# Attention's maximum pass as pairs of 64-row products, the second half's keys stored swapped, and one of eight high parts made by VectorE

## What is computed

```python
q = (x @ Wq.T).reshape(b, t, N_HEADS, HEAD_DIM)          # 8 heads of 64
kv_latent = x @ Wkv_down.T                               # 64 latent columns
k = (kv_latent @ Wk_up.T).reshape(b, t, N_HEADS, HEAD_DIM)
v = (kv_latent @ Wv_up.T).reshape(b, t, N_HEADS, HEAD_DIM)
scores = jnp.einsum('bqhd,bkhd->bhqk', q, k) * scale
attn = jax.nn.softmax(scores, axis=-1)
out = jnp.einsum('bhqk,bkhd->bqhd', attn, v)
return out.reshape(b, t, N_HEADS * HEAD_DIM) @ Wo.T
```

## Time and profile before

| | |
|---|---|
| median of three runs (lowest to highest) | 1378.51 us (1374.25 to 1379.99) |
| profiled execution | 1377.57 us |
| its span, first to last instruction | 1375.6 us |
| busy over the span: TensorE, VectorE, ScalarE, GpSimd | 1219.7, 1145.5, 1054.7, 962.1 us |
| attention's loop in the span | from about 502 to 1140 us |

### The profile page before, as it was taken

One profiled execution on the slowest core, in us unless ns is written; L12 is line 12 of the kernel. 1 busy time (PEld: TensorE's weight loads), 2 busy tenths in 40 slices (PEclk: granted clock), 3 DMA queues, 4 the chain that ended last, 5 costly groups with the idle time before them and its releaser, 6 DMA issues.

```text
span 1375.6 us, 30660 instructions
## 1 busy us (share of the span) xinstructions
PE 1219.7 (89%) x10192; PEld 745.8 (54%) x10192; DVE 1145.5 (83%) x3141; ACT 1054.7 (77%) x2351; POOL 962.1 (70%) x1100
## 2 busy tenths in 40 slices
PE   3999999867888879999999999999999999677776
PEld 1455555434455536665666666666666667344443
DVE  6999998589998888888777787877878754799998
ACT  3332333677899869999999989999999995787776
POOL 4456644368777777778777778777777773388887
PEclk9899999989999999999999999999999999799998
DMA  6200000000012000010000000000000000000000
GB/s 174 77 1 1 0 0 1 1 1 1 10 38 78 27 21 25 25 26 25 25 14 14 2 2 2 2 3 2 2 2 2 2 3 1 1 31 16 25 22 32
DMA packets 35529, 25.32 MB, mean 18 GB/s; under 512 B 16358, under 2 KB 32044, under 8 KB 35372
## 3 DMA queue, kind: packets, MB, share of 16 engines
q1 hardware_dynamic: 35372, 23.36, 6.0%
HBM read 14.89 MB, written 8.39 MB: 17 GB/s over the span
## 4 chain that ended last, share of the span: by engine, by line
PE 58%; ACT 13%; issue 12%; DVE 11%; POOL 4%; DVEq 0%; DMA 0%; SPq 0%; POOLq 0%; ACTq 0%
PE banks L2023 7%; PE banks L2025 6%; PE banks L2011 6%; DVE arena L1535 4%; PE banks L1761 4%; PE banks L1969 4%; PE banks L1720 4%; PE banks L2040 4%; PE banks L2041 4%; PE banks L2042 3%; ACT arena L1174 3%; DVE arena L1530 3%; ACT arena L1182 2%; PE banks L1748 2%; PE banks L1776 2%
## 5 line engine op out<-in xcount | busy, mean ns | idle before, releaser
L839 POOL TENSOR_TENSOR arena<-arena 128x512 f16<-128x512 f32 x383 | 437.6, 1161 | 150.5 <-ACT arena L1182 146.6
L1174 ACT ACTIVATE arena<-banks 128x512 f32<-128x512 f32 x512 | 302.9, 599 | 45.5 <-PE banks L2025 40.8
L1611 DVE TENSOR_REDUCE arena<-banks 128x1 f32<-128x512 f32 x512 | 325.8, 680 | 4.0 <-PE banks L2011 1.8
L1182 ACT ACTIVATE arena<-arena 128x512 f16<-128x512 f32 x512 | 316.2, 632 | 0.0
L1530 DVE MAX8 arena<-arena 128x8 f32<-128x256 f32 x512 | 190.4, 414 | 27.4 <-issue 15.9
L2040 PE MATMUL banks<-arena 128*128 128x65 f16 x2016 | 211.4, 193 | 0.9
L2041 PE MATMUL banks<-arena 128*128 128x64 f16 x2016 | 211.5, 195 | 0.0
L2042 PE MATMUL banks<-arena 128*128 128x65 f16 x2016 | 210.6, 193 | 0.0
L1637 DVE TENSOR_TENSOR arena<-arena 128x512 f16<-128x512 f32 x129 | 107.0, 829 | 123.2 <-ACT arena L1182 123.0
L1535 DVE MATCH_REPLACE8 arena<-arena 128x256 f32<-128x256 f32 x512 | 206.2, 411 | 0.9 <-issue 0.2
L2040 PEld LDWEIGHTS banks<-arena 128*128 128x128 f16 x2016 | 187.9, 96 | 31.8 <-issue 9.9
(11 more groups left out here) (229 smaller groups left out, 2545.1 us busy)
## 6 DMA issues: line engine op xcount, KB each, us to landing
arena<-q_store SPq DMA_DIRECT2D x48, 128.0 KB, 2.7
x<-in_L_attn_a_x SPq DMA_DIRECT2D x8, 512.0 KB, 3.9
q_store<-arena SPq DMA_DIRECT2D x32, 128.0 KB, 1.8
out<-x SPq DMA_DIRECT2D x7, 512.0 KB, 2.9
arena<-arena SPq DMA_DIRECT2D x64, 1.0 KB, 1.9
arena<-in_L_attn_a_W_in SPq DMA_DIRECT2D x1, 768.0 KB, 5.8
arena<-in_L_attn_a_W_mid SPq DMA_DIRECT2D x1, 512.0 KB, 7.6
arena<-in_L_attn_a_w_w SPq DMA_DIRECT2D x2, 256.0 KB, 8.0
```

What stands on the lines that cost most here:

```text
L839: nc.gpsimd.tensor_tensor(pr_lo[c][:, kt, :], pr[:, kt, :], pr_hi[c][:, kt, :], ALU.subtract).then_inc(a_lP, 1)
L1174: nc.scalar.activation(pr[:, kt, :], ps[6 + kt % 2][:, :], ACT.Exp, scale=SM_SCALE).then_inc(a_P, 1)
L1182: nc.scalar.activation(pr_hi[c][:, kt, :], pr[:, kt, :], ACT.Copy).then_inc(a_hi, 1)
L1611: nc.vector.tensor_reduce(mx_half[c][:, i // 2, i % 2:i % 2 + 1], ps[n % MAX_BANKS][:, :], X, ALU.max).then_inc(a_mx, 1)
```

## The change

Each two maximum products become a pair, `max_pair(W, j)`, issued in steps 0, 2, 4 and 6. Either product uses 64 of the 128 rows: the first half of the keys in partitions 0 to 63, the second half in 64 to 127. To that end the second half of the keys is stored with high and low parts swapped, so that its high parts are in 64 to 127; the score products, which sum over all rows, are not changed by the order. The maximum is now one of high parts by high parts only. The pair waits once, until the bank of its second product has been read. The latent rows, which are made from the keys by a transpose, are copied in two pieces for the second half to undo the swap. Apart from that the high part of step 3 is made by VectorE (`high`, in step 4 between the reduction and the subtraction) instead of ScalarE, with a semaphore of its own on which GpSimd's subtraction of step 3 waits.

```diff
+        HIGH_DVE = 3
+
+        def high_done(W, kt):
+
+            if kt == HIGH_DVE:
+                return W + 1
+            return W * (KT - 1) + kt + (kt < HIGH_DVE)
...
+        def low_half(c):
+
+            return slice(HD, P) if c == 0 else slice(0, HD)
...
             def low(W, kt):
                 c = W % 2
-                pool.wait_ge(a_hi, W * KT + kt + 1)
+                pool.wait_ge(a_hiD if kt == HIGH_DVE else a_hi, high_done(W, kt))
                 nc.gpsimd.tensor_tensor(pr_lo[c][:, kt, :], pr[:, kt, :], pr_hi[c][:, kt, :],
                                         ALU.subtract).then_inc(a_lP, 1)
...
             def latent(B, c, bank):
                 act.wait_ge(a_lps, B * 2 + c + 1)
-                nc.scalar.activation(lat[B % 2][:, c * TPC:c * TPC + TPC, 1:1 + 2 * HD],
-                                     ps[bank].bitcast(F16)[:, 0:TPC * P].rearrange("p (t d) -> p t d", t=TPC),
+                rows = ps[bank].bitcast(F16)[:, 0:TPC * P].rearrange("p (t d) -> p t d", t=TPC)
+                tiles = slice(c * TPC, c * TPC + TPC)
+                if c == 0:
+                    nc.scalar.activation(lat[B % 2][:, tiles, 1:1 + 2 * HD], rows, ACT.Copy).then_inc(a_l, 1)
+                    return
+                nc.scalar.activation(lat[B % 2][:, tiles, 1:1 + HD], rows[:, :, HD:P], ACT.Copy)
+                nc.scalar.activation(lat[B % 2][:, tiles, 1 + HD:1 + 2 * HD], rows[:, :, 0:HD],
                                      ACT.Copy).then_inc(a_l, 1)
...
                     exps(W, kt)
-                    if kt:
+                    if kt and kt - 1 != HIGH_DVE:
                         high(W, kt - 1)
...
             def keys_low(B, c, bank):
                 cs = slice(c * CH, c * CH + CH)
                 dve.wait_ge(a_k, ((B - AHEAD) * 2 + c) * 2 + 2)
-                nc.vector.tensor_tensor(kA[B % 2][HD:P, cs], ps[bank][HD:P, :], kA[B % 2][HD:P, cs],
+                low = low_half(c)
+                nc.vector.tensor_tensor(kA[B % 2][low, cs], ps[bank][low, :], kA[B % 2][low, cs],
                                         ALU.subtract).then_inc(a_kl, 1)
...
+            def high(W):
+
+                dve.wait_ge(a_P, W * KT + HIGH_DVE + 1)
+                wait_from(dve, a_ops, W - 1)
+                nc.vector.tensor_copy(pr_hi[W % 2][:, HIGH_DVE, :], pr[:, HIGH_DVE, :]).then_inc(a_hiD, 1)
...
                     if W + 2 < ALL:
                         largest_of(W + 2, kt)
+                    if kt == HIGH_DVE + 1:
+                        high(W)
                     if kt in (LAST_DVE if W == ALL - 1 else LOW_DVE):
                         low(W, kt)
...
-            def max_scores(W, i):
+            def max_pair(W, j):
 
                 B, hh, c, slot = place(W)
-                j, half, n = i // 2, i % 2, W * HALVES + i
...
-                wait_from(pe, a_mx, n - MAX_BANKS + 1)
+                wait_from(pe, a_mx, n + 1 - MAX_BANKS + 1)
                 every = qA[:, slot, c * CH:c * CH + CH].rearrange("p (q j) -> p j q", j=TPC)
-                mm(ps[n % MAX_BANKS][:, :], every[:, j, :], kA[B % 2][:, half * CH:half * CH + CH],
-                   start=True, stop=True).then_inc(a_mps, 1)
+                for half in range(2):
+                    high = slice(HD * half, HD * half + HD)
+                    mm(ps[(n + half) % MAX_BANKS][:, :], every[high, j, :], kA[B % 2][high, half * CH:half * CH + CH],
+                       start=True, stop=True).then_inc(a_mps, 1)
...
                     scores(W, kt)
-                    if W + 2 < ALL:
-                        max_scores(W + 2, kt)
+                    if W + 2 < ALL and kt % 2 == 0:
+                        max_pair(W + 2, kt // 2)
```

More of the change, by code:

```diff
@@ L337, in hybrid_block_kernel @@
         a_hi = sem("a_exp_high")
+        a_hiD = sem("a_exp_high_vector")
         a_lD = sem("a_exp_low_dve")
@@ L1210, in head_second @@
                         act.wait_ge(h_kmps, k + 1)
-                        nc.scalar.activation(kA[B][HD:P, c * CH:c * CH + CH], ps[bank][HD:P, :],
+                        low = low_half(c)
+                        nc.scalar.activation(kA[B][low, c * CH:c * CH + CH], ps[bank][low, :],
                                              ACT.Copy).then_inc(a_kl, 1)
@@ L1635, in low @@
                 c = W % 2
-                dve.wait_ge(a_hi, W * KT + kt + 1)
+                dve.wait_ge(a_hi, high_done(W, kt))
                 nc.vector.tensor_tensor(pr_lo[c][:, kt, :], pr[:, kt, :], pr_hi[c][:, kt, :],
                                         ALU.subtract).then_inc(a_lD, 1)
+            def high(W):
+                dve.wait_ge(a_P, W * KT + HIGH_DVE + 1)
+                wait_from(dve, a_ops, W - 1)
+                nc.vector.tensor_copy(pr_hi[W % 2][:, HIGH_DVE, :], pr[:, HIGH_DVE, :]).then_inc(a_hiD, 1)
             def head(t):
@@ L1997, in slot_work @@
                     read[slot] = (s_zT, (LN_ATTN + n * 2 + part[0]) * 2 + part[1] + 1)
-            def max_scores(W, i):
+            def max_pair(W, j):
                 B, hh, c, slot = place(W)
-                j, half, n = i // 2, i % 2, W * HALVES + i
-                if i == 0:
+                n = W * HALVES + 2 * j
+                if j == 0:
                     pe.wait_ge(a_kl, B * 2 + 2)
-                if i == 0 and B < AHEAD:
+                if j == 0 and B < AHEAD:
                     pe.wait_ge(s_qld, (B * NH + hh + 1) * 48)
-                if i == 0 and B >= AHEAD:
+                if j == 0 and B >= AHEAD:
                     pe.wait_ge(a_dup, query_done(W))
-                wait_from(pe, a_mx, n - MAX_BANKS + 1)
+                wait_from(pe, a_mx, n + 1 - MAX_BANKS + 1)
                 every = qA[:, slot, c * CH:c * CH + CH].rearrange("p (q j) -> p j q", j=TPC)
-                mm(ps[n % MAX_BANKS][:, :], every[:, j, :], kA[B % 2][:, half * CH:half * CH + CH],
-                   start=True, stop=True).then_inc(a_mps, 1)
+                for half in range(2):
+                    high = slice(HD * half, HD * half + HD)
+                    mm(ps[(n + half) % MAX_BANKS][:, :], every[high, j, :], kA[B % 2][high, half * CH:half * CH + CH],
+                       start=True, stop=True).then_inc(a_mps, 1)
             def scores(W, kt):
@@ L2101, in head_second @@
                     pe.wait_ge(f_lg, NT)
-                    for i in range(2):
-                        max_scores(0, i)
+                    max_pair(0, 0)
                     pe.wait_ge(*head_read[2])
-                    for i in range(2, HALVES):
-                        max_scores(0, i)
+                    for j in range(1, TPC):
+                        max_pair(0, j)
             ffn(0)
-            for i in range(HALVES):
-                max_scores(1, i)
+            for j in range(TPC):
+                max_pair(1, j)
             pe.wait_ge(f_fs, NT + CREDIT["f_fs"])
```

## The result

The changed kernel takes 1428.48 us (1426.01 to 1429.18), against 1377.57 in the runs beside it: 1.037 times as long, interval 1.034 to 1.039. The forecast was 1381, its range ended at 1397. The profiled execution's span grew from 1375.6 to 1426.9 us, by 51.3. Of that, 45.8 lie in the 64 items of attention's loop: from the first score product of its first step to the first of its last step it lasts 673.8 us, before 628.0. Another 3.4 lie ahead of the loop, which starts at 505.42 instead of 502.00.

A forecast was written before the change was run, and what follows sets the result against it. TensorE was taken to bound the kernel, with ScalarE hardly behind in items without other work. Terms 3.4 - 0.5 - 1.7 + 2.9 - 0.5 = +3.6 us on 1377.57 gave 1381 us; range 1355 to 1397.

The forecast's parts named there:

- The pair's wait: Ahead of a pair, for two of three banks: +0.6 us in about 5 items behind row statistics, +2.9 us.
- Rival C: Wait for two banks, steps 0, 2, 4, 6: pairs wait for VectorE's reductions, +17, 1395 us; chance 0.14.
- The price of a pair: Pair between full-width products, division changing twice: 0.45 us against 0.43, +0.02; +3.4 us in 41 items.
- A: In the pairs: changing the array's division costs nothing, a pair saves 0.2 us, result 1337 us; chance 0.13.
- B: In the pairs: changing the array's division costs half, a pair at 0.34 us, result 1363 us; chance 0.15.
- D: In the pairs: the two halves don't overlap, a pair at 0.67 us, result 1437 us; chance 0.05.
- The high part at 0: VectorE's copy in step 4, 0.44 to 0.83 us, is covered by its idle time before the subtraction: cost 0.
- Items without other work: 17 loop items without queries or output products: -0.1 us each, between -0.31 and +0.08; -1.7 us in all.
- The clock: TensorE's clock at its lower level between 503 and 1153 us, named as a sign of a wrong forecast; unpriced.
- the first two maximum passes: Before 502 us: paced by VectorE's reductions and ending with the same wait, so 0.

The follow-up runs named there:

- the last four kernels: Full products in pairs, subtractions moved (1386.02 us); changed kernel, own bank waits (1425.89); kernel before, VectorE's low part of chunk 6 for 4 (1377.51), plus its high part (1405.87).
- the first experiment: Changed kernel with the high part of step 3 back on ScalarE, pairs kept: 1416.59 us, 1.027 times the kernel before.
- the kernel of 1396.59 us: Changed kernel with all high parts on ScalarE and VectorE's two subtractions moved behind the reductions of steps 2 and 6: 1396.59 us, 1.014.
- the last kernel above: Kernel before with VectorE making the low parts of chunks 0 and 6 instead of 0 and 4, and chunk 6's high part: 1405.87 us, 1.021.

## Why the prediction was wrong

The steps from the kernel before to the changed one, each the difference of two medians: 1377.0 us before (the runs beside the last four kernels); +9.1 for grouping full products in pairs, order mended; +10.6 for making them halves; +20.0 for the order of VectorE's subtractions; +11.9 for the high part on VectorE. Together 1428.5. In the loop of the profiled executions the same four steps are 9.5, 5.4, 21.6 and 9.3, together the 45.8.

*The pair's wait* is the step that failed. It was sized at +0.6 us in 5 items behind row statistics, +2.9 us, on the ground that "in most items the reductions run ahead". The pairs wait 45.2 us, in items of every kind: the kernel with full products in pairs, whose array is never divided, still lost 46 us; 12 of them, by the first experiment, to the high part. The statement "the pair waits where the second waited" was wrong about the time: the second product used to ask for its bank a step later. To let the first product start on its own bank gave back 2.6 us; to ask a step later gave back 26, and to take VectorE's subtractions from ahead of the reductions 20 and 28.5. The earlier trace rows showed single products hardly waiting, not what two at once would need. Rival C had this mechanism and named the threshold (over 25 us on the weight loads; 67.3 came), but at half a reduction of 0.6 us once in an item, +17. Its place was right; its size was a third, since it counted VectorE's added work and not the waits ahead of the reductions.

*The price of a pair* was 0.45 against 0.43 us, +0.02; it is +0.05. The parts that the prediction listed were right: the starts in the kernel of 1396.59 us, where nothing waits, are (lines 2054 and 2056 the score products, 2042 the pair, 1998 the output products)

```profile
663.46 0.38 PE L2056 MATMUL banks<-arena 128*128 128x512 f16 x1
663.77 0.41 PE L2042 MATMUL banks<-arena 64*128 64x512 f16 x2
664.11 1.13 PE L1998 MATMUL banks<-voB,arena 128*128 128x256 f32 x4
665.07 0.38 PE L2054 MATMUL banks<-arena 128*128 128x512 f16 x1
...
665.50 1.03 PE L1998 MATMUL banks<-voB,arena 128*128 128x256 f32 x4
666.37 0.38 PE L2054 MATMUL banks<-arena 128*128 128x512 f16 x1
```

0.31 from the score product to the pair and 0.34 from the pair to the next start; less the 0.215 that the score product streams, the pair takes 0.435, where 0.45 was forecast. But behind the pair come f32 products, in steps 0 and 2 of these items: they take 0.96 us until the next product may start, the same four without a change ahead of them 0.87. This exposed load was read in the earlier trace rows (0.33 for 0.27) and then left out of the sum, which took the f16 weights of the earlier trace rows. The pair of step 0 then costs 0.525; with that of step 2, which has f32 transposes behind it, this is most of the 0.19 an item. The Trainium skill, "TensorEngine Tiling (Array Packing)", Key Properties, says that a change of mode drains TensorE; the 0.1 us on either side agree. Rivals A and B, which gave the change away or half of it, and D, in which the halves don't overlap, fell.

*The high part at 0* failed too: +8 us alone, +12 with the pairs. The cover that was named, VectorE's idle time ahead of its subtraction, is there, but GpSimd is the one that pays: its subtraction of step 3 waited 43 us for the copy, in 61 of the 64 items, and "the next subtraction waits for ScalarE anyway" covers less than half of that. With the copy alone, the subtraction of step 5 still waits 33.9 us for ScalarE, in 40 items, where it waited 53.5 in 46 before. The bound on the copy's time was right in the mean (589 ns, of 414 to 1217; forecast 0.44 to 0.83), from the group of line 1663:

```profile
L1663 DVE CAST arena<-arena x64: 414/577/1217, 512.2 to 1176.8; 128x512 f16<-128x512 f32 x64
```

Neither saving a copy on ScalarE (its busy time in the loop fell) nor the idle of VectorE was worth anything here, as neither was what the items waited for.

*Items without other work*, -0.1 each by forecast, take +0.62. With the order mended, 8.78 with halves and 8.76 with full products: here the division costs nearly nothing, since ScalarE sets the pace, and the bound of +0.08 was exceeded by the pairs' places alone. The remaining 0.22 to 0.24 come at the place where the earlier trace rows show ScalarE waiting 0.26 us for TensorE: in step 4 a pair (0.43 us) now stands ahead of the score products of step 5, where a single product (0.215) stood, and ScalarE waits 0.46 us there with halves (at 571.55) and 0.47 with full products:

```profile
569.05 0.60 ACT L1190 ACTIVATE arena<-banks 128x512 f32<-128x512 f32 x1 [0.47 <-PE banks L2055]
```

*The clock.* The prediction named a lower clock between 503 and 1153 us as a sign that it was wrong, and it came. Busy times after, and TensorE's timeline there:

```profile
665.00:668.00 3.00, 3.00 (x10) 1.18 (x10) 2.10 (x7) 1.98 (x4) 1.59 (x5) 0.50 0.00 0
```

```profile
664.55 0.41 PE L2040 MATMUL banks<-arena 64*128 64x512 f16 x2 [1.95 <-DVE arena L1630]
664.89 0.61 PE L2052 MATMUL banks<-arena 128*128 128x512 f16 x1
665.29 0.63 PE L2054 MATMUL banks<-arena 128*128 128x512 f16 x1
```

Behind a pair's wait of 1.95 us the granted clock is at 0.50, the 1.2 GHz level, for about 3 us, and the next product starts 0.40 us behind the one before it instead of 0.215. This is an item behind row statistics; at 698.03 and 876.09 a wait of 1.95 us has the same behind it. These are the three longest waits of pairs in the loop; the fourth, 1.88 us at 839.99, has no lower clock behind it. Together these stretches are some 10 us at the lower level, which costs at most 5. Before, there is no such stretch from 503 to 1153 us, and with full products and the mended order there is none in the loop after 504. So these three go with the waits; the item at 695.49 lost 2.3 us by both, where +0.6 had been forecast for its kind.

A fourth stretch is older than the pairs' waits. In the changed kernel the clock is at its lower level from 487.4 us, ahead of the first pair at 492.70, to 508; before, it is at 1.00 from 488 to 510.

```profile
503.00:507.00 4.00, 2.74 (x9) 0.54 (x10) 3.75 (x7) 0.45 (x1) 0.00 (x0) 0.50 0.00 0
```

So the first two maximum passes, sized at 0, last 12.7 us up to the loop instead of 9.4. In the kernel with full products in pairs and the mended order, where the clock was at its upper level for most of this stretch, they last 10.0: most of the 3.3 us goes with the clock, and why it fell there is not known.

## What to carry to other kernels

A product that needs two buffers at once has a wait of its own, even if the work is the same: before grouping, go through the queue of the engine that frees the buffers and ask what each freeing instruction stands behind. Where an engine in the middle of a cycle has slack, the slack is no cover for those who wait for it; put its instructions that wait for others behind the ones that release the bound engine, as here, where that order alone gave back 20 and 28.5 us. Whether a fourth bank would have done the same was not tried. Half-array products between full-width ones gave nothing back here: two halves side by side cost 0.05 us more than two full products.

## What the runs showed of the hardware

VectorE and GpSimd disturb each other. In the kernel before, VectorE's subtraction of 512 elements takes 680 to 693 ns in the 38 cases in which no subtraction of GpSimd overlaps it, and 829 in the mean of 129. In the last kernel above, 25 of 129 lie wholly beside GpSimd's, with a median of 1526 ns; the copy from f32 to f16, 412 ns at its fastest, has a median of 953 in 35 cases wholly beside them. VectorE's reductions from PSUM take 680 ns in the mean before and 681 after, and 680 in the median of the 246 that lie wholly beside GpSimd's subtractions.

The records show a wait and not a lower rate. In the last kernel, each of the 80 VectorE subtractions of over 1 us began while one of GpSimd's ran and ended 0.54 to 0.55 us after that one's end (the one at 578.40 above ends at 579.93, and GpSimd's row ends at 579.38). It goes the other way too: 93 of GpSimd's 95 subtractions of over 1.25 us (1.15 at the fastest) began while VectorE's copy or subtraction ran, and ended 1.01 to 1.03 us after its end. The Trainium skill, "SBUF — State Buffer", Who interferes with whom, says that the two engines share a pair of ports as an exclusive lock, which a VectorE instruction takes that has two SBUF inputs or runs in a two-port mode, and that a reduction doesn't; the later of the two is blocked until the other is through. The three durations and the ends agree. By that rule a copy moved from ScalarE to VectorE beside a busy GpSimd is not a copy of 0.44 us, and that reading was missing from the prediction.

A change of the array's division that divides only the rows costs 0.10 us ahead of a 64-row product and 0.12 behind it, at the upper clock, and up to 0.09 more where f32 weights follow. One 64-row product alone in each step costs 0.255 us more than a full one, in the mean of the eight of an item, three of them with f32 behind.
